# Third layer's router in a four-layer kernel: the expert choice in two halves, scatters and place reads put elsewhere, counts in five operations

## The reference

```python
logits = xt @ Wg + bg                                  # (2048, 8), xt = layernorm of x
probs = jax.nn.softmax(logits, axis=-1)
gate_vals, exp_idx = jax.lax.top_k(probs, 2)
gate_vals = gate_vals / jnp.sum(gate_vals, axis=-1, keepdims=True)
capacity = int(np.ceil(1.2 * T * 2 / 8))               # 615 (T is 2048)
eidx = exp_idx.T.reshape(-1)
oh = jax.nn.one_hot(eidx, 8, dtype=jnp.int32)
pos = jnp.sum((jnp.cumsum(oh, axis=0) - oh) * oh, axis=-1)
keep = pos < capacity
...
h = jax.nn.gelu(jnp.einsum('ecd,edf->ecf', buf, W1) + b1[:, None, :], approximate=True)
ye = jnp.einsum('ecf,efd->ecd', h, W2) + b2[:, None, :]
```

## Time and profile before

| | |
|---|---|
| median of 3 runs | 1185.39 us (1182.25 to 1188.87) |
| the profiled execution | 1184.15 us, span 1182.4 us |
| busy in the span | PE 82%, PEld 69%, DVE 53%, ACT 47%, POOL 33% |
| mean granted clock of PE | 0.899 of 2.4 GHz |
| third layer's attention with its router | about 535 to 739 us of the span |
| fourth layer's attention with its router | about 880 to 1029 us |

### The profile page before, as it was taken

The page is one execution under the profiler, slowest core; times in us unless marked ns, Lnnn a source line. Parts: engine busy times, 40 slices in busy tenths (PEclk is TensorE's granted clock), DMA queues, the critical chain, the costliest instruction groups (busy, mean ns, idle before and its releaser), DMA issues. The chain is left out here.

```text
span 1182.4 us, 20612 instructions
## 1 busy us (share of the span) xinstructions
PE 964.0 (82%) x7766; PEld 812.5 (69%) x7766; DVE 624.7 (53%) x1721; ACT 549.8 (47%) x1053; POOL 391.1 (33%) x382
## 2 busy tenths in 40 slices
PE   4888899999988999968897884889248876299992
PEld 3565799999977899946665663889226655288882
DVE  7876321211157533377888854344377775444443
ACT  1665534344442444446675541655325552155552
POOL 4444201000013110410100345356555447545552
PEclk9999899999995999999999965899768997599997
DMA  9999930000000000000000001766200001445543
GB/s 346 166 169 168 165 93 1 1 1 1 1 1 1 1 1 1 1 1 2 1 2 1 17 24 46 224 188 207 79 0 2 1 1 37 122 150 185 165 154 107
DMA packets 70577, 83.83 MB, mean 71 GB/s; under 512 B 5297, under 2 KB 57528, under 8 KB 70352
## 3 DMA queue, kind: packets, MB, share of 16 engines
q1 hardware_dynamic: 64336, 71.98, 27.1%
q0 software_dynamic: 4992, 8.45, 2.1%
q10 hardware_dynamic: 1152, 2.10, 0.5%
HBM read 52.15 MB, written 32.18 MB: 71 GB/s over the span
## 5 line engine op out<-in xcount | busy, mean ns | idle before, releaser
L2225 ACT ACTIVATE hT<-PS,par 128x512 f32<-128x512 f32 x200 | 136.5, 688 | 179.2 <-PE PS L2173 177.6
L2265 DVE SCALAR_TENSOR_TENSOR X<-PS,wts,X 128x128 f32<-128x128 f32 x272 | 76.5, 344 | 226.2 <-PE PS L2185 226.2
L1066 ACT ACTIVATE hT<-PS 116x512 f32<-116x512 f32 (+1 forms) x192 | 101.9, 560 | 100.9 <-PE PS L847 99.7
L847 PE MATMUL PS<-par,score 128*116 128x128 f32 x704 | 111.6, 297 | 21.0 <-DVE oc L972 9.0
L2185 PEld LDWEIGHTS PS<-regA,hT 128*128 128x128 f32 x1024 | 119.2, 192 | 2.8
L2185 PE MATMUL PS<-regA,hT 128*128 128x128 f32 x1024 | 119.4, 275 | 0.0
L847 PEld LDWEIGHTS PS<-par,score 128*116 128x116 f32 x704 | 82.8, 146 | 37.9 <-issue 29.3
L1134 POOL TENSOR_TENSOR score<-score,mx 128x1232 f32<-128x1232 f32 x32 | 72.0, 2249 | 101.8 <-DVE mx L952 101.8
L1936 PE MATMUL PS<-q_up,halves 128*112 128x256 f32 (+1 forms) x276 | 85.8, 311 | 8.8 <-DVE hT L2048 8.7
L2171 PE MATMUL PS<-x_up,w_halves 128*128 128x512 f32 x200 | 86.4, 432 | 0.0
L1043 ACT ACTIVATE score<-score 128x1232 f32<-128x1232 f32 x64 | 78.3, 1223 | 13.2 <-POOL score L1134 10.9
(11 more groups left out here) (305 smaller groups left out, 2021.3 us busy)
## 6 DMA issues: line engine op xcount, KB each, us to landing
regA<-L3f_w SPq DMA_DIRECT2D x23, 704.0 KB, 4.2
regB<-L2f_w SPq DMA_DIRECT2D x23, 578.0 KB, 4.0
L2f_sorted_x<-empty_row SPq DMA_DIRECT2D x8, 1161.0 KB, 22.1
L3f_sorted_x<-empty_row SPq DMA_DIRECT2D x8, 1161.0 KB, 22.6
regA<-L0f_w SPq DMA_DIRECT2D x4, 768.0 KB, 17.3
regA<-L2f_sorted_x SPq DMA_DIRECT2D x23, 129.0 KB, 3.8
regB<-L3f_sorted_x SPq DMA_DIRECT2D x23, 129.0 KB, 4.0
par<-params SPq DMA_DIRECT2D x1, 2450.0 KB, 14.7
```

The source lines that it names most:

```text
L847: last = nc.tensor.transpose(PS[0:BW, bank_of(("exps", 3 * u + i)), (j % 4) * P:(j % 4) * P + P], exps_of(u)[:, first:first + BW], ident)
L1066: nc.scalar.activation(hT[0:BW, u % 2, i, 0:width], PS[0:BW, bank, 0:width], ACT.Copy).then_inc(pT_ready.sem, 1)
L2225: nc.scalar.activation(hT[:, n % 2, k, :], PS[:, i % 4, :], c["act"], bias=pc(f"{tag}_b1")[:, col:col + 1]).then_inc(h_ready.sem, 1)
```

## The change

For the third layer: `choose` is cut into `choose` (best expert) and `choose_second` (second expert and counts); the table moves the steps; the second half stands one unit of work behind the first. The ranks and places of parts 0 and 1 come an iteration later, and the places of part 2 leave the loop and stand in `late_vector` behind the last `apply`. On POOL the scatters of tile steps 10 to 13 come ahead of the power of the row norm, and the five scatters at step 14 leave the loop: three stand ahead of the last power and two behind it. For both sparse layers the counts of part 0, eight tiles, are made by a copy, three additions over both groups of four tiles, and one addition of the first group's total onto the second.

```diff
-                            choose=(21, 29, 33), ranks=(22, 30, 34), place=(23, 31, 35)),
+                            choose=(21, 29, 33), second=(22, 30, 33), ranks=(23, 31, 34), place=(24, 32)),
...
-                            choose=(13, 17), ranks=(13, 17), place=(14, 19)),
+                            choose=(13, 17), second=(13, 17), ranks=(13, 17), place=(14, 19)),
...
+            def choose_second(v, st, part):
+                t0, t1 = parts[part]
+                rest = picks[:, 2, 0:t1 - t0, :]
+                nc.vector.scalar_tensor_tensor(rest, onehots[:, 0, t0:t1, :], -3.0e38, logits_of[:, t0:t1, :], ALU.mult, ALU.add)\
+                    .then_inc(v_step, st.one())
+                v.wait_ge(v_step, st.n)
+                first_of_max(v, st, part, rest, 1)
                 if part == 0:
                     nc.vector.memset(earlier_sum[:, :, 0, :], 0.0).then_inc(v_step, st.one())
+                    if t1 == 2 * TG:
+                        oh = onehots[:, :, 0:t1, :].rearrange("p a (h j) e -> p a h j e", h=2)
+                        total = earlier_sum[:, :, 1:t1 + 1, :].rearrange("p a (h j) e -> p a h j e", h=2)
+                        nc.vector.tensor_copy(total[:, :, :, 0, :], oh[:, :, :, 0, :]).then_inc(v_step, st.one())
+                        v.wait_ge(v_step, st.n)
+                        for j in range(1, TG):
+                            nc.vector.tensor_tensor(total[:, :, :, j, :], total[:, :, :, j - 1, :], oh[:, :, :, j, :], ALU.add)\
+                                .then_inc(v_step, st.one())
+                            v.wait_ge(v_step, st.n)
+                        nc.vector.tensor_tensor(total[:, :, 1, :, :], total[:, :, 1, :, :],
+                                                total[:, :, 0, TG - 1, :].unsqueeze(2).to_broadcast([P, 2, TG, E]), ALU.add)\
+                            .then_inc(oh_ready.sem, 1)
+                        return
...
             def vector_between(v, st, u):
+                if tag == "L2f" and due("second", u) == 1:
+                    choose_second(v, st, 1)
...
             def vector_end(v, st, u):
                 if tag == "L2f" and due("choose", u) is not None:
                     choose(v, st, due("choose", u))
+                if tag == "L2f" and due("second", u) in (0, 2):
+                    choose_second(v, st, due("second", u))
...
             def pool_tile(p, st, t):
+                if tag == "L2f" and 10 <= t < 14:
+                    pool_scatter(p, 0, range(4 * (t - 10), 4 * (t - 9)))
                 g, left = divmod(t - (8 if tag == "L3f" else 3), TG)
                 if left == 0 and 0 <= g < (2 if tag == "L3f" else 3):
                     pool_power(p, g)
                 if tag == "L2f":
-                    if 10 <= t < 14:
-                        pool_scatter(p, 0, range(4 * (t - 10), 4 * (t - 9)))
                     if t == 13:
                         pool_power(p, 3)
-                    if t == 14:
-                        pool_scatter(p, 1, range(0, 5))
...
             def late_vector(v, st):
                 apply(v, st, late)
+                if tag == "L2f":
+                    place(v, st, last_part - 1, ranks_bank[last_part - 1])
                 read_logits(v, st, late, 1)
                 choose(v, st, last_part)
+                choose_second(v, st, last_part)
...
             def late_pool(p, st):
+                if tag == "L2f":
+                    pool_scatter(p, 1, range(3))
                 pool_power(p, late)
                 if tag == "L3f":
                     pool_scatter(p, 1, range(2 * TG))
                 else:
-                    pool_scatter(p, 1, range(5, 8))
+                    pool_scatter(p, 1, range(3, 8))
                     pool_scatter(p, 2, range(4))
                 pool_scatter(p, last_part, range(2 * (parts[-1][1] - parts[-1][0])))
```

More of the change, by code:

```diff
@@ L1532, in tensor_ranks @@
             def tensor_ranks(pe, part, bank):
+                ranks_bank[part] = bank
                 t0, t1 = parts[part]
@@ L1587, in read_logits, with first_of_max @@
                         .then_inc(logits_read.sem, 1)
-            def choose(v, st, part):
+            def first_of_max(v, st, part, src, i):
                 t0, t1 = parts[part]
@@ L1615, in choose @@
-                first_of_max(lg, 0)
-                nc.vector.scalar_tensor_tensor(rest, onehots[:, 0, t0:t1, :], -3.0e38, lg, ALU.mult, ALU.add).then_inc(v_step, st.one())
+                m, oh = top[:, i, t0:t1], onehots[:, i, t0:t1, :]
+                nc.vector.tensor_reduce(m, src, AX.X, ALU.max).then_inc(v_step, st.one())
+                v.wait_ge(v_step, st.n)
+                nc.vector.tensor_tensor(eq, src, over_e(m), ALU.is_equal).then_inc(v_step, st.one())
+                v.wait_ge(v_step, st.n)
@@ new lines, in first_of_max, with choose @@
+                nc.vector.scalar_tensor_tensor(key, eq, -1000.0, iota, ALU.mult, ALU.add).then_inc(v_step, st.one())
+                v.wait_ge(v_step, st.n)
+                nc.vector.tensor_reduce(kmin, key, AX.X, ALU.min).then_inc(v_step, st.one())
+                v.wait_ge(v_step, st.n)
+                nc.vector.tensor_tensor(oh, key, over_e(kmin), ALU.is_equal).then_inc(v_step, st.one())
+                v.wait_ge(v_step, st.n)
+            def choose(v, st, part):
+                t0, t1 = parts[part]
+                v.wait_ge(logits_read.sem, logits_read.at(groups_before(t1)))
+                first_of_max(v, st, part, logits_of[:, t0:t1, :], 0)
@@ L1668, in vector_start @@
                     choose(v, st, due("choose", u))
+                if tag == "L3f" and due("second", u) is not None:
+                    choose_second(v, st, due("second", u))
                 if due("place", u) is not None:
```

20 lines of the change are left out of this document (5 added, 15 removed).

## The result

The changed kernel takes 1174.11 us (median of 4 runs, 1171.49 to 1176.24) against 1185.28 (4 runs). The medians are 11.17 apart; the ratio recorded for the pair is 0.992, 95% interval 0.9892 to 0.9947. The profiled execution took 1176.24, 7.91 less than that of before; it is the slowest of the four. In lines, scatters are now L1719, the choice L1603 to L1622, the new counts L1631 to L1637, the places L1658 to L1670, weight loads L1904 and row loads L1910.

The account below looks back on a forecast made before the run. The third layer's loop was taken as bound by a ring of engines briefly waiting for each other. Gains summing to 7.75 us take the profiled 1184.15 to 1176.4; the median, 1.24 above, gives 1177.6, range 1171.5 to 1185.

Parts of the forecast that it names:

- X: Third layer's loop: the step from the start of PE's transposes to the next residual (L994); 3.40 us at full clock.
- c: Third layer, from iteration 28's residual to part 1's choice: full clock if PE doesn't wait, gain 1.9 us (0 to 1.9).
- d: Part 1's choice in halves, from its start to PE's transposes: gain 2.1 us (1.5 to 2.4).
- a: Part 0's choice in two halves, iterations 21 to 24: PE's transposes start earlier, gain 1.7 us (1.0 to 2.7).
- e: Clock of 697 to 701, around iteration 30's transposes to residual: gain 0 us (0 to 1.3 if clock is full).
- f: Ranks and places of part 1 an iteration later, behind unit 31's weighted values: gain 0.3 us (-1.3 to +1.9).
- b: POOL's scatters ahead of the row norm's power, ending ACT's wait for `osr` in iteration 28: gain 1.25 us (0.9 to 1.96).
- g: End of the sort: logits earlier, but POOL's scatters set the row load, 4.49 behind the last: gain 0 us (-0.1 to +1.3).
- The rival of the scatters (B): Scatters become the sort's end and weight loads share their transfers: 2 to 5 us of gain lost, 1181 to 1183; chance 0.10.
- h: Fourth layer's counts of part 0, five operations for eight additions: gain 0.5 us (0 to 0.6).
- The rival of the clock (A): Clock stays low despite shorter waits: gain only 4.35 us (3 to 5.9), time 1181.0; chance 0.24.
- The slower case (D): New pause of 2.2 us throws the clock down through iterations 23 to 28: 8.9 us slower, 1194; chance 0.05.

Follow-up runs that it names:

- Choices in one piece: Changed kernel with both halves of the choices of parts 0 and 1 in one piece again, at the end of iterations 21 and 29: 1179.18 us, ratio 0.9964.
- scores computed thrice: Changed kernel with PE computing unit 25's scores in the third layer three times, filling its new wait in iteration 23: 1172.07 us, ratio 0.9908.
- the end as before: Changed kernel with part 2's places inside the loop again and five scatters at tile step 14: 1180.63 us, ratio 0.9988.
- powers first: Changed kernel with POOL's scatters of tile steps 10 to 13 behind the row norm's power again: 1174.07 us, ratio 0.993.
- counts alone: Kernel before with only part 0's counts made in five operations, in both sparse layers: 1184.85 us against 1183.07, ratio 1.0005.
- rows ahead of weights: Changed kernel with unit 25's scores three times and, in both sparse layers, the first two weight loads behind the first two row loads: 1193.16 us, ratio 1.0011.

## Why the prediction was right, and which of its steps were not

The sign was right, and the forecast of 1177.6 stands 3.5 above the median measured. The steps on which most of the sum rested came out in size: PE's transposes in iteration 22 came 7.67 behind the X of 20 (7.6 by the forecast's 642.6), the new wait was 2.18 (2.2), the five counts 1.10 (1.15), c 1.93 (1.9) and d 2.06 (2.1). Choices in one piece confirm a plus d and e at about 4. But that the profiled pair's 7.91 stands so close to the sum of 7.75 is partly luck: misses of both signs met, and the medians are 11.17 apart. Of the 7.91, experiments tie 3.9 to the halves, 0.6 to the end, about nothing to POOL's order and to the counts; what brings c and f, 4.2 together, isn't isolated by any. On the third chip the same change brought nothing that can be measured.

**a** was 1.04 and not the 1.7 taken: the clock fell behind the new wait of 2.18. That is the lower bound of 1.0, but this bound was not what its own terms give: from 660.1, the last two steps (0.97 and 3.40 are 4.4, not 5.0) grow by 1.7 at the factor 1.39 and the ranks by 0.8, which makes 662.6 and a gain of 0.2, not 661.8 and 1.0. With 0.2 the lower ends would sum to 1.2. That the X of 24 came 26.77 behind that of 20, where 661.8 makes 26.8, is luck. The scores computed thrice show that this fall costs 2.16; so with a full clock the term would have been 1.04 + 2.16 = 3.2, above its upper bound of 2.7.

**b** failed in the changed profile: 0.46 over two X steps instead of 1.25, and no loss when undone. The price of the wait, 1.25, agrees with 13.23 to 13.30 against 12.02, but only at full clock. That a clock fall would replace the wait is what the prediction left out; where it didn't (five profiles), X 26 to 28 is 12.0. The step also missed what the POOL edit is needed for. Places that come an iteration later hold up the five scatters of step 14, which stand ahead of the last `osr`; unless these leave the loop, as they do, 4.7 of the gain are lost in the last X step, as the end as before showed. The prediction priced these scatters only against the late power.

**c** had its size right, and its cause isn't settled. The prediction put the fall at 684 down to ACT's wait. Where that wait is gone, the fall is gone too; but in powers first the wait is back and the fall doesn't come. What the rows allow is narrower: in the kernel before and in counts alone the wait met a full clock and the fall followed (c is 7.57 in both); in powers first the clock fell between 679 and 680, as it did in the changed kernel without the wait, and was back at 683. No run has the wait at full clock in the changed loop. Of the signs listed beside **d**, 1.9 behind the start of part 1's choice is PE's transposes (1.87); `normalise` itself began 1.11 behind it.

**e and f** were taken as 0 and 0.3 and gave 1.35 and 2.25. e was the bound named for full clock. f has two courses: 13.58 or 13.59 from the X of 30 to the last one in the changed profile and in five others, and 16.19 to 16.49 in two kernels with the same loop and in the changed kernel on the third chip; the granted clock from the X of 30 to that of 32 is 0.99 or 1.00 with the first and 0.65 to 0.68 with the second. What chooses between them isn't shown. The second course is a loss of 0.4 to 0.7 against 15.83, within the range given, as its f said.

**g** took the row load for bound by the last scatter, at 4.49 behind it. That reading of the earlier trace rows was wrong: it followed SP's weight load by 3.10, and that `tile_at`; in the changed profile it stands 3.72 behind the last scatter, not 4.5. The earlier `apply` brought 0.64, which the end as before took back. The last power did wait for the three scatters ahead of it, but for 0.2 only: it began 0.48 behind the variances (710.37) where it had begun 0.30 behind. The rival of the scatters (B) has its mechanism, as rows ahead of weights showed. Where weights and last scatter meet, the last X to the row load is 22.37 to 22.89 (four profiles) instead of 21.42, 1.0 to 1.5 more and also more than the 22.06 of before; so g is +0.64 or down to -0.8, beyond the -0.1 given. It did not decide.

**h** had the wrong sign. The operations became shorter by 0.54 as reckoned, and PE's wait by 0.66; by the third reading of logits the fourth layer had lost 1.74, and its next interval gave back 0.75. Eight additions in place of five undo both. The granted clock between the readings (0.76 against 0.87) goes with it in all ten profiles of the first two chips; why shorter counts bring it down isn't shown.

**The rival of the clock** (A) was half right: the clock did fall in iteration 23, and in 28 in some executions, but not for all of the later stretch. The slower case (D) did not come. Its 0 for c came in no changed kernel on the first two chips, where the X of 28 to the choice of part 1 is 5.64 to 5.66 in all eight. On the third chip, with its "remote" waits, none of the cases describes what was seen; whether the kernel before has fewer of these waits there was not profiled, and stays open.

## What to carry to other kernels

A wait in such a ring can be paid twice, once as itself and once by what PE's clock does behind it (here 2.16 behind a wait of 2.18). Price the second at both levels, and look whether a few products that nobody needs, put where PE would wait, are cheaper. Compare stretches between the same two instructions, and read the granted clock over each of them: here a removed wait and a fall of the clock hid each other. Where a step is moved later, list what stands behind it on the queues that wait for it: here 4.7 of the gain depended on five scatters that had to move too. And "B comes 4.5 behind A" in one row does not say that B waits for A: compare the distance to the other things that B waits for, in a second place or a second kernel.

## What the runs showed of the hardware that was not expected

Redundant work made a stretch shorter: with 24 more products in a wait, the X of iteration 24 comes 13.57 behind that of 22 instead of 15.73, at a granted clock of 1.00 instead of 0.76. All four profiles with these products show it (13.57 or 13.58), on two chips. By the times alone it isn't shown: 1172.07 beside 1174.39 on the same chip, with overlapping intervals.

The same two kernels differed by 0.8% on one chip and by nothing measurable on another (0.992, 0.9892 to 0.9947, and 0.9993, 0.9975 to 1.0012), where DVE and ACT waited 15 to 29 us per execution for "remote", all but two of 33 times in the stretches in which POOL scatters. That these waits cost the gain isn't shown, since the kernel before was not profiled there.

Stretches that no edit touches move by more than most edits here: from the third layer's row load to the fourth layer's first reading of logits it is 199.90 to 202.74 in the profiles of the first two chips, and from the fourth layer's row load to the end 149.08 to 150.72, without relation to the edits. A difference of 1 us can be read from neighbouring rows of a trace, but not from the times.
